# Last layer of a four-layer network: six first-pass units and the values ahead of the router's chain

## The reference

```python
def _L3_attn_ref(x, W_qkv, b_qkv, W_out, b_out):      # x: (4, 1024, 128), 16 heads of 8
    qkv = (x @ W_qkv + b_qkv).reshape(b, s, h, 3 * hd)
    ...
    logits = jnp.einsum('bshd,bkhd->bhsk', q, k) / np.sqrt(hd)
    logits = jnp.where(mask[None, None, :, :], -jnp.inf, logits)     # causal
    attn = jax.nn.softmax(logits, axis=-1)
    out = jnp.einsum('bhsk,bkhd->bshd', attn, v).reshape(b, s, d)
    return out @ W_out + b_out

def _L3_ffn_ref(x, router_w, w1, b1, w2, b2):
    router_probs = jax.nn.softmax(x_flat @ router_w.T, axis=-1)      # 4096 tokens, 8 experts
    top_k_probs, top_k_idx = jax.lax.top_k(router_probs, 2)
    ...
    for e in range(E):
        h = new_gelu(x_flat @ w1[e].T + b1[e])
        out_e = h @ w2[e].T + b2[e]
        output = output + cw[:, e:e + 1] * out_e
```

## Time and profile before

| | us |
|---|---|
| median of 3 runs | 2266.37 |
| lowest and highest run | 2261.76, 2266.69 |
| profiled execution: span from first to last instruction | 2265.1 |
| this stage begins in the span at about | 1472 |
| PE, DVE, ACT, POOL busy over the span | 1884.8, 1796.7, 1381.4, 1293.2 |

### The profile page before, as it was taken

One profiled execution on the slowest core, in us unless ns is written; L12 is line 12 of the kernel. 1 busy time (PEld: TensorE's weight loads), 2 busy tenths in 40 slices (PEclk: granted clock), 3 DMA queues, 4 the chain that ended last, 5 costly groups with the idle time before them and its releaser, 6 DMA issues. The chain is left out here.

```text
span 2265.1 us, 32659 instructions
## 1 busy us (share of the span) xinstructions
PE 1884.8 (83%) x10276; PEld 999.3 (44%) x10276; DVE 1796.7 (79%) x2181; ACT 1381.4 (61%) x2604; POOL 1293.2 (57%) x954
## 2 busy tenths in 40 slices
PE   5798988889898987788985899955688988888886
PEld 5333333334343433344662688842244544445432
DVE  6699999899989999967879899868656665566673
ACT  2666767666767675465353787631476666766666
POOL 5689999999999999801333445446511111111265
PEclk6999999999999999899987899955899999999998
DMA  3355444445545555420030000022422332223112
GB/s 77 109 157 152 156 146 158 149 153 161 159 146 159 152 157 158 134 86 30 1 91 0 1 0 0 0 62 82 120 67 76 111 107 83 80 84 108 57 34 76
DMA packets 156309, 217.53 MB, mean 96 GB/s; under 512 B 31722, under 2 KB 68602, under 8 KB 155546
## 3 DMA queue, kind: packets, MB, share of 16 engines
q1 hardware_dynamic: 152074, 207.41, 30.3%
q0 software_dynamic: 4096, 8.40, 1.4%
HBM read 196.59 MB, written 23.86 MB: 97 GB/s over the span
## 5 line engine op out<-in xcount | busy, mean ns | idle before, releaser
L1035 POOL TENSOR_TENSOR m_dBx<-m_du,m_rowB 128x1024 f32<-128x1024 f32 x256 | 603.8, 2386 | 9.9 <-DMA m_rowB<-bc_rows 9.8
L758 PE MATMUL ps<-m_hC,ident 128*128 128x512 f32 x1024 | 517.2, 652 | 104.5 <-DVE m_hC L1117 104.2
L3195 DVE TENSOR_REDUCE a_mx<-ps 128x2 f32<-128x1024 f32 (+2 forms) x320 | 350.8, 1117 | 141.3 <-PE ps L2757 105.0
L2985 ACT ACTIVATE a_pT<-ps 128x512 f32<-128x512 f32 (+2 forms) x640 | 318.7, 558 | 225.6 <-PE ps L2780 199.4
L934 ACT ACTIVATE ps<-m_delta,m_A 128x512 f32<-128x512 f32 x512 | 332.8, 682 | 144.9 <-DVE m_hC L1117 113.1
L758 PEld LDWEIGHTS ps<-m_hC,ident 128*128 128x128 f32 x1024 | 205.4, 208 | 398.9 <-issue 238.3
L3356 POOL TENSOR_SCALAR_AFFINE_SELECT a_pT<-a_pT 128x512 f32<-128x512 f32 x104 | 66.1, 635 | 431.1 <-ACT a_pT L2985 430.8
L1117 DVE TENSOR_TENSOR m_hC<-ps,m_rowC 128x1024 f32<-128x1024 f32 x176 | 215.4, 1224 | 16.7 <-issue 1.3
L1108 DVE TENSOR_TENSOR_SCAN ps<-ps,m_dBx 128x1024 f32<-128x1024 f32 x88 | 201.1, 2285 | 30.0 <-POOL m_dBx L1035 16.6
L1045 POOL TENSOR_TENSOR m_hC<-m_h,m_rowC 128x1024 f32<-128x1024 f32 x80 | 194.6, 2432 | 45.2 <-DVE m_h L1108 45.0
L1108 DVE TENSOR_TENSOR_SCAN ps<-ps,m_carry,m_dBx 128x1024 f32<-128x1024 f32 x88 | 206.4, 2345 | 5.4 <-ACT m_dBx L959 4.5
(11 more groups left out here) (410 smaller groups left out, 3510.9 us busy)
## 6 DMA issues: line engine op xcount, KB each, us to landing
m_rowB<-bc_rows SPq DMA_DIRECT2D x256, 256.0 KB, 3.9
m_rowC<-bc_rows SPq DMA_DIRECT2D x256, 256.0 KB, 3.4
a_w<-in_L3f_w1T SPq DMA_DIRECT2D x39, 256.0 KB, 2.8
a_w<-in_L3f_w2T SPq DMA_DIRECT2D x39, 256.0 KB, 3.7
expert_rows<-in_zero_rows SPq DMA_DIRECT2D x39, 128.0 KB, 2.7
a_xs<-expert_rows SPq DMA_DIRECT2D x39, 128.0 KB, 2.9
expert_out<-a_y SPq DMA_DIRECT2D x39, 128.0 KB, 3.6
qk_parts<-a_part SPq DMA_DIRECT2D x18, 256.0 KB
```

Of the source, the lines that this page charges most:

```text
L758: mm = pe.matmul(ps[:, bankY + c, :], k.ident[:], hC[:, n % NBUF, c, :], start=False, stop=n % NS == NS - 1)
L1035: pool.tensor_tensor(dBx[:, n % NBUF], du[:, i % 2, :, chunk(i, x)], rowB[:, n % 4, :].unsqueeze(1).to_broadcast([P, HALF, CH]), ALU.mult) ...
L2985: act.activation(dst, src, ACT.Exp).then_inc(t_read, 1)
L3195: dve.tensor_reduce(mx[:, c % 2, :, es[0]:es[0] + len(es), t, x // CH], src, AX_X, ALU.max)\
```

## The change

The first six units of item 0 are done before DVE's `route` and before the loop; the values of the first sequence are projected between the fourth and fifth routed block, not behind the seventh; the last routed block stands between units 1 and 2; the router's logits go into `bankO`, which is zeroed only after DVE has copied them out, so the ring's entry `("G",)` is gone; and `count` and `slots` stand at `g` = 4 of slot 0, behind units 6 and 7, not at `g` = 0 behind units 0 and 1. `count` waits for the second expert's one-hot and not for the last weight.

```diff
+EARLY = 6
+def units_of(s, g):
+    return range(max(sum(SHARE[:g]), 0 if s else EARLY), sum(SHARE[:g + 1])) if s < NI else ()
...
     project(0, 2)
-    add(s_at, ("G",))
+    for i in range(EARLY):
+        add(s_at, ("S", 0, i))
...
-            units = range(sum(SHARE[:g]), sum(SHARE[:g + 1])) if s < NI else ()
+            units = units_of(s, g)
...
-            if s == 0 and g == 0:
+            if s == 0 and g == 4:
                 add(s_at, ("C",))
...
 # PE
                 def route(i):
-                    bank = take_s("G")
                     pe.wait_ge(t_read, t_at["N", i] + 1)
                     for j in range(4 * i, 4 * i + 4):
-                        mm = pe.matmul(k.ps[:, bank, j * NE:j * NE + NE], k.xnT[:, j * P:j * P + P], gw[:],
+                        mm = pe.matmul(k.ps[:, bankO, j * NE:j * NE + NE], k.xnT[:, j * P:j * P + P], gw[:],
                                        start=True, stop=True)
                     if i == NCH - 1:
-                        mm.then_inc(s_done, 1)
+                        mm.then_inc(routed, 1)
                 def count():
                     bank = take_s("C")
-                    when(pe, VR, "cw1")
+                    when(pe, VR, top2_names("r")[-1])
...
                 for i in range(3, NCH):
                     turn_normed(i)
+                    if i == 4:
+                        project(0, 2)
                     route(i - 1)
-                project(0, 2)
+                pe.wait_ge(ready, 9)
+                for i in range(2):
+                    score(0, i)
                 route(NCH - 1)
-                pe.wait_ge(ready, 9)
+                for i in range(2, EARLY):
+                    score(0, i)
                 pe.wait_ge(o_zero, 1)
...
-                        if s == 0 and g == 0:
+                        if s == 0 and g == 4:
                             count()
 # DVE
                 statistics(1)
-                dve.memset(k.ps[:, bankO, :], 0.0).then_inc(o_zero, 1)
...
                 def route():
-                    bank = arrived("G")
-                    logit = k.ps[:, bank, 0:NT * NE].rearrange("p (t e) -> p t e", e=NE)
+                    dve.wait_ge(routed, 1)
+                    logit = k.ps[:, bankO, 0:NT * NE].rearrange("p (t e) -> p t e", e=NE)
                     step(VR, dve.tensor_copy(pr, logit), "logit")
-                    dve.sem_inc(s_read, 1)
+                    dve.memset(k.ps[:, bankO, :], 0.0).then_inc(o_zero, 1)
...
                 values(0)
+                dve.wait_ge(mx_zero, 1)
+                for i in range(EARLY):
+                    largest(0, i)
                 route()
-                dve.wait_ge(mx_zero, 1)
...
-                        if s == 0 and g == 0:
+                        if s == 0 and g == 4:
                             slots()
```

More of the change, by code:

```diff
@@ L2538, in attn3_stage @@
         bias_scaled, turned_one = k.sem("a3_bias_scaled"), k.sem("a3_ones_column")
-        router_exp = k.sem("a3_router_exp")
+        router_exp, routed = k.sem("a3_router_exp"), k.sem("a3_router_done")
         deviations, normed = k.sem("a3_deviations"), k.sem("a3_normed")
@@ L2898, in _ @@
                     for g in range(GROUPS):
-                        units = range(sum(SHARE[:g]), sum(SHARE[:g + 1])) if front else ()
+                        units = units_of(s, g)
                         if back:
@@ L3279, in _ @@
                     for g in range(GROUPS):
-                        units = range(sum(SHARE[:g]), sum(SHARE[:g + 1])) if first < NI else ()
+                        units = units_of(s, g)
                         for i in units[:1]:
```

## The result

The changed kernel takes 2273.27 us in the median of 22 runs (2264.21 to 2283.09), the kernel before 2263.53 in 22 runs beside it (2256.64 to 2271.89). The ratio is 1.0042, 95% interval 1.0029 to 1.0056: **slower by 0.42%**, 9.5 us (6.6 to 12.7). The forecast was 2271.1 us, 4.7 above 2266.37, the median of the three runs of before then known; its range ended at 2273.0, just under the median. The 22 runs put the kernel before 2.8 lower than those three, so the change costs twice what was forecast for it, 9.5 and not 4.7 us.

The account below looks back on a forecast made before the run. POOL's 64 unbroken scatters bound the kernel, as they release the load of the first expert tile. The first scatter moves from 1536.64 to 1541.35, passed on whole: 2266.4 + 4.7 = 2271.1 us, range 2267.5 to 2273.0.

Parts of the forecast that it names:

- The line to the first scatter: Router, `count`, `slots`, then POOL in the last stage: no spare time, first scatter 4.7 us later, at 1541.35.
- the zeroing: Clearing `bankO` leaves the start of DVE's stream: worth 0 to 0.48 us, taken as 0.25; adds 0.48 inside the router's chain.
- the bytes: DMA traffic from 1510 to 1526, 1152 kB, nearly matches the stores behind item 0's stacks, so the stacks landed by about 1510.0.
- The rivals on the stacks and the clock: Item 0's stacks landing at 1507.9: +2.6 us, chance 0.13; at 1511.17: +6.1, 0.08; TensorE kept at 2.4 GHz: +1.9, 0.10.
- Passing it on: From first scatter to first expert tile: POOL never runs short, so everything from slot 3 on moves by 4.7 us.
- the sum: Steps up to the first scatter added together: 1541.35 - 1536.64 = 4.7 us later.
- The wait ahead of the tile: PE's pause before the first expert tile, at the head of slot 3: grows from 9.97 to about 13 us.
- the late stacks: Rival: item 0's stacks land at 1511.17, with no gain from the zeroing: +6.1 us, 2272.5, chance 0.08.
- inner range: The main forecast's own range, 2270.0 to 2272.3 us, at chance 0.55.
- the three terms named for it: Zeroing 0 to 0.48 us, stack landing half a microsecond either way, POOL's start of the first scatter 0.30 to 0.86.
- the line: About 0.2% (4.5 us), what a measurement of this kernel can tell from no change; slower lies above 2270.9 us.
- the line that has spare time: The front line, first-pass units of items 0, 1 and 2 on DVE: has the spare 9.97 us.

Follow-up runs that it names:

- last layer: Layers 0 to 2 left out of each kernel: before 827.23 us, changed 835.97, with POOL's scatters delayed 835.27, with values and scatters earlier 821.03.
- cut kernels: Layers 0 to 2 and all work behind the first expert tile left out: before 202.33 us, changed 209.99, with POOL's scatters delayed 210.25.
- the delayed one: Kernel before with nothing moved, but four clears of an unused buffer on POOL ahead of its first scatter: 2271.77 us, ratio 1.0040.
- the second profile: Changed kernel run once more, unedited, against the kernel before: 2274.15 us in 12 runs, ratio 1.0044.
- the two earlier variants: Kernel before with values earlier and first scatter not waiting for unit 3: 2261.49 us; the same plus `count` and `slots` ahead of the first pass: 2260.29.

## Why the prediction was half right

**The line to the first scatter** was right step by step. Counted from each stage's start, the prediction put the first scores at 1509.75 - 1472.34 = 37.4; they ran at 1505.78 - 1468.05 = 37.7. From there to the router's first step it had 8.3, the trace has 1514.10 - 1505.78 = 8.3; the router with the zeroing 10.1 against 10.0; from the router's end to `count` 1.26 against 1.28; `count` to DVE's copy 3.81 against 3.82; to the row numbers' end 7.28 against 7.27; to the scatter 0.86 against 0.89. The only term that was off is the start. The stack loads went out 0.48 sooner (33.15 after the stage's start against 33.63), in this pair the whole price of the zeroing and not half of it; in the three other pairs they went out 0.86, 0.57 and 0.00 sooner, so that the zeroing moved them is likely and not shown. But the last one was used 1505.78 - 1501.52 = 4.3 after its issue ended, where the bytes had given 3.7. Net 0.3: 5.0 late in this pair of profiles instead of 4.7, and 5.2 in the mean of the four pairs that share this start (whole kernel twice, last layer, cut kernels). A slip in the working changes little: 1.68 + 1.72 is 3.4, not 3.3.

**The rivals on the stacks and the clock** fell. Scores as early as 1507.9 - 1472.34 = 35.6 did not come, nor as late as 1511.17 - 1472.34 = 38.8. The routed block took 1.87 (1.72 before) and `count` to its copy 3.82 (3.81 before), and the granted clock stayed at 0.50 there. The windows of the changed kernel (us, PE, PEld, DVE, ACT, POOL, clock, DMA share, GB/s):

```profile
1505.70:1514.00 8.30, 6.31 (x56) 4.37 (x56) 5.91 (x6) 0.00 (x0) 0.00 (x0) 0.50 0.20 76
1525.00:1529.20 4.20, 3.85 (x8) 1.31 (x10) 1.46 (x3) 0.00 (x0) 0.00 (x0) 0.50 0.37 112
```

**"Passing it on" is the step that failed.** It took the 4.7 to the tile one for one, with a series of scatters that keeps its 84.8. POOL's line is indeed without a pause, but its turns do not have fixed lengths: they depend on what DVE does beside them. The kernel before shows it too, with a scatter of 1.86. A later start shifts POOL's split of the maxima onto DVE's two subtractions, and in three of the four profiles of the changed timetable, and in all three of the delayed one, the turn with the split takes 4.9 to 5.0 instead of 3.1. In the first profile of the changed kernel it is a scatter that meets them instead (2.00 instead of 0.96, at 1568.50), as before, so that this profile agrees with the sum by luck. The prediction asked whether POOL runs short of units, and never what stands beside POOL's own work at its new place. Shown by taking it away: 1.9 ± 1.2 us, where the prediction had nothing.

The Trainium skill, page "SBUF — State Buffer", section "Who interferes with whom", states this rule: the port pair that VectorE and GpSimd share is an exclusive lock, and a VectorE instruction with two SBUF inputs contends for it with a GpSimd instruction that reads SBUF. The trace agrees: the held steps end 0.28 behind the first and 0.15 behind the second subtraction. The prediction did not weigh it, and should have.

**The wait ahead of the tile** grew, as it had to if the scatters end it: 9.97 to 11.76 and, in the second profile, to 15.1; 13 was forecast. It is counted from when PE is through with the slots before it, and so varies with them.

**The sum and the range.** First scatter some 5.2 to 5.6 instead of 4.7, collision 1.9: about 7.5 at the tile, measured directly in the cut kernels. This is inside the interval of the whole kernel (6.6 to 12.7). Whether the rest of the median's 9.5 is more than its spread stays open. Behind the tile the profiles take 631.0 to 638.4 us with the kernel before and 633.9 to 635.1 with the changed one, and the last layer alone gives 8.4 ± 2.7. TensorE's mean granted clock there was 0.97 in the shortest of these stretches and 0.96 in the longest. The range ended at 2273.0 because it allowed the late stacks, half a microsecond for the spread, and nothing for a series that stretches. Its inner range, 2270.0 to 2272.3, does not come out of the three terms named for it, which give 2269.8 to 2271.9. The chance of slower (0.46) was held down by a sum that lay right at the line.

**Why it does not pay** is the forecast's own reason: six units fill a hole of DVE on the line that has spare time, and stand ahead of a router that the tile waits for. The trace has the router's chain begin at 46.0 after the stage's start and not at 38.6. The run with `count` right behind the router and the two earlier variants bear it out, though none moves the six units alone. The router in the hole, with scatters that no longer wait for unit 3, gave the tile 6 to 7 us.

## What to carry to other kernels

When a line of back-to-back work moves, its length is not a constant: look at what the other engines do beside each of its turns at the new place, above all VectorE's instructions with two SBUF inputs beside GpSimd's. Where two lines meet at a wait, fill a hole with work of the line that has no slack. To size a few microseconds in 2,270, cut the kernel behind the event in question and time that.

## What the runs showed of the hardware

- An indirect scatter on POOL took 2.00 instead of 0.96 us when a pair of DVE's subtractions (128x1024, two inputs, 2.35 for the two) began 0.09 before it, and splitting steps on 32x128 took 1.17 to 1.41 instead of 0.28 to 0.42 beside them. With subtractions of 32 columns the same steps took 0.28 and 0.42 again. The delay goes both ways: beside held steps of the split a subtraction took up to 1.46 instead of 1.22.
- The values' products, moved from a stretch with a granted clock of 0.50 into one that was granted 1.00, took 1.95 instead of 3.76 us. The prediction counted this move at nothing, and nothing on the path hung on it.

```profile
1487.80:1489.80 2.00, 2.00 (x20) 1.86 (x17) 2.00 (x8) 1.82 (x3) 0.00 (x0) 1.00 0.17 41
```
